# Decoder layer, last batch of the first stage: step sizes and sums in another order, part of the work in the next stage

## The reference

```
x = x + attention(layernorm(x))            # 16 heads of 32, 2 key/value heads, causal softmax
x = x + mamba(context, layernorm(x))       # selective scan over the context, gated by silu of the normed x
x = x + experts(layernorm(x))              # 16 experts, two chosen per token, and a shared one
```

```
c  = silu(conv4(in_proj(context)) + conv_b)         # 512 channels x 512 steps
dt_low, B, C = split(x_proj(c))                     # 16 rows each
dt = softplus(dt_proj(dt_low) + dt_b)               # 512 x 512
q, k, v = projections of layernorm(x)
state = state * exp(dt * A) + (dt * c) * B          # A = -exp(a_log), 16 states per channel; y = sum(state * C) + D * c
```

## Time and profile before

| | us |
|---|---|
| median of three runs | 1198.75 |
| profiled execution | 1197.57 |
| its span in the profile | 1195.8 |
| first stage, to the start of the second | 171.07 |
| second stage, to its last attention tile at 679.7 | 508.6 |
| the rest | 516.1 |

### The profile page before, as it was taken

The page is one execution under the profiler, slowest core; times in us unless marked ns, Lnnn a source line. Parts: engine busy times, 40 slices in busy tenths (PEclk is TensorE's granted clock), DMA queues, the critical chain, the costliest instruction groups (busy, mean ns, idle before and its releaser), DMA issues. The chain is left out here.

```text
span 1195.8 us, 18629 instructions
## 1 busy us (share of the span) xinstructions
PE 1072.8 (90%) x6368; PEld 641.9 (54%) x6368; DVE 808.5 (68%) x1199; ACT 666.1 (56%) x1438; POOL 672.2 (56%) x587
## 2 busy tenths in 40 slices
PE   7999928888888888888888899999999989999993
PEld 3444415655656665656656544544444456666651
DVE  5478769999999999999999567740680133323327
ACT  3566669999999999999999424202011022222210
POOL 1033269999999999999999640202043034444420
PEclk9999959999999999999999999999999999999997
DMA  6210001101111111112232123112225423333229
GB/s 211 90 37 19 13 15 36 37 32 32 36 36 37 37 32 32 37 36 72 80 100 70 58 85 106 68 38 70 71 72 205 162 88 125 125 130 127 69 73 367
DMA packets 51932, 94.74 MB, mean 79 GB/s; under 512 B 9918, under 2 KB 18110, under 8 KB 51840
## 3 DMA queue, kind: packets, MB, share of 16 engines
q1 hardware_dynamic: 44320, 72.82, 18.4%
q0 software_dynamic: 7520, 20.72, 5.3%
HBM read 74.51 MB, written 20.84 MB: 80 GB/s over the span
## 5 line engine op out<-in xcount | busy, mean ns | idle before, releaser
L604 POOL TENSOR_TENSOR w_all<-w_all 128x512 f32<-128x512 f32 x256 | 320.3, 1274 | 0.6 <-POOLq L96 0.3
L782 DVE TENSOR_TENSOR_SCAN w_all<-da,w_all 128x512 f32<-128x512 f32 x256 | 297.8, 1205 | 0.0
L716 ACT ACTIVATE da<-w_all,a_flat 128x512 f32<-128x512 f32 x256 | 180.2, 704 | 9.0 <-PEq L96 7.7
L683 PE MATMUL yb<-ident,w_all 128*128 128x128 f32 x1024 | 159.8, 279 | 21.0 <-DVE acc L790 21.0
L633 PE MATMUL sc<-w_all,attn 32*128 32x384 f32 (+3 forms) x512 | 105.0, 486 | 45.5 <-ACT w_all L724 22.8
L724 ACT ACTIVATE w_all<-sc,neg_max 128x128 f32<-128x128 f32 (+3 forms) x256 | 134.2, 540 | 15.0 <-DVE neg_max L774 13.9
L683 PEld LDWEIGHTS yb<-ident,w_all 128*128 128x128 f32 x1024 | 115.0, 141 | 45.4 <-issue 24.3
L1199 POOL TENSOR_TENSOR w_all<-w_all 128x512 f32<-128x512 f32 x24 | 29.4, 1226 | 165.0 <-ACT w_all L1396 165.0
L774 DVE TENSOR_REDUCE neg_max<-sc 128x2 f32<-128x256 f32 (+3 forms) x128 | 104.1, 813 | 24.1 <-PE sc L636 20.1
L733 ACT ACTIVATE w_all<-tb 128x256 f32<-128x256 f32 (+2 forms) x192 | 102.9, 536 | 22.6 <-PE tb L648 22.6
L1261 PE MATMUL pc<-w_all 128*128 128x512 f32 x256 | 112.1, 593 | 0.0
(11 more groups left out here) (198 smaller groups left out, 1679.1 us busy)
## 6 DMA issues: line engine op xcount, KB each, us to landing
w_all<-b_scratch SPq DMA_DIRECT2D x64, 256.0 KB, 3.3
w_all<-in_w_up SPq DMA_DIRECT2D x16, 512.0 KB, 5.4
w_all<-in_w_down SPq DMA_DIRECT2D x16, 512.0 KB, 6.6
w_all<-sorted_y SPq DMA_DIRECT2D x16, 512.0 KB, 10.9
attn<-in_x SPq DMA_DIRECT2D x4, 1024.0 KB, 7.4
w_all<-in_x SPq DMA_DIRECT2D x16, 256.0 KB, 4.0
norms<-attn SPq DMA_DIRECT2D x4, 1024.0 KB, 4.3
out_dram<-acc SPq DMA_DIRECT2D x16, 256.0 KB, 8.9
```

Of the source, the lines that this page charges most:

```text
L604: pool.tensor_tensor(dbu[:, k, :], keep["du"][i // N][:, k * T:(k + 1) * T], b_all[i % 2][:, :], ALU.mult).then_inc(pool_dbu.sem, pool_dbu ...
L683: last = pe.transpose(yb[which][:, k * P:(k + 1) * P], state[i % 2][:, k, t * P:(t + 1) * P], ident[:, :])
L716: act.activation(da[unit % 2][:, :], keep["dt"][i // N][:, k * T:(k + 1) * T], ACT.Exp, scale=keep["a_flat"][:, unit % (N * KD):unit % (N ...
L782: dve.tensor_tensor_scan(state[i % 2][:, k, :], da[unit % 2][:, :], dbu[:, k, :], 0.0, ALU.mult, ALU.add).then_inc(dve_scan.sem, dve_scan. ...
```

## The change

For the last batch (LAST = 3) of the first stage only, unless said otherwise:

- TensorE: after three of four query tiles the step rows, then at once the step sizes, then keys and values (into bank 0), the fourth query tile, the skip transposes (banks 1, 2, 5, 6), C, V. V's and C's transposes and the skip's are functions of their own, called for the other batches in the old order.
- The normalized x goes to `w_in` and `ctx_t` instead of `acc`, and the skip term to `xp` instead of `dt`'s tile, so that their new neighbours can write those.
- The step rows are copied by VectorE and not ScalarE.
- Abs reads the step sizes from PSUM with the bias in the instruction; the biased value for the sum is computed on VectorE after it.
- The sums, in all batches, are max(z, 0) - lost, ahead of the logarithm, and + ln behind it; 1 + e and lost alternate.
- exp(a_log) and a_flat are computed in the loop's second iteration.
- The fourth query tile's scaling, the skip copies and the C and V copies are at the end of ScalarE's stream.
- SyncE stores the B rows ahead of the keys' spreading.
- GpSimd's four products dt * c move into the second stage, one each in its steps 0 to 3.

```diff
+        def skipped(b, j):
+            return xc(b, j) if b < LAST else xp[:, j, TAPS - 1:]
+        def skip_bank(b, l):
+            return bank[l] if b < LAST else bank[(1, 2, 5, 6)[l]]
@@ sync: the last batch's rows before its keys @@
+                if b < B - 1:
+                    spread_keys(b)
...
                 sp.dma_start(d["b_rows"][b, :, :], rows[R:R + N, :]).then_inc(s_b.sem, s_b.tick(b))
+                if b == B - 1:
+                    spread_keys(b)
@@ gpsimd @@
-            weigh(B - 1)
@@ tensor @@
+                for m in range(3 if b == B - 1 else 4):
+                    query(b, m)
+                if b < B - 1:
+                    key_value(b)
+                step_rows(b)
+            steps(LAST)
+            key_value(LAST)
+            query(LAST, 3)
+            turn_skip(LAST)
+            turn_c(LAST)
+            turn_v(LAST)
-            tail(B - 1)
+            def steps(b):
...
+                else:
+                    pe.wait_ge(act_xt.sem, act_xt.upto(4 * b + 3))
+                    pe.wait_ge(dve_rows.sem, dve_rows.upto(0))
                 for j in four:
                     pe.matmul(bank[4 + j][:, :], w_dt4[j * DH:j * DH + R, j * P:(j + 1) * P], rows[j * DH:j * DH + R, :],
@@ scalar @@
             def exponent(b):
...
+                    else:
+                        act.wait_ge(pe_dt.sem, pe_dt.upto(4 * b + j))
+                        act.activation(ex[:, j, :], bank[4 + j][:, :], ACT.Abs, bias=dt_b[:, j:j + 1]).then_inc(act_abs.sem, act_abs.tick(4 * b + j))
...
+                if b == 0:
+                    act.wait_ge(s_rest.sem, s_rest.upto(6))
+                    act.activation(a_log[:, :, :], a_log[:, :, :], ACT.Exp).then_inc(act_alog.sem, act_alog.tick(0))
...
-            skip(B - 1)
-            exponent(B - 1)
-            logarithm(B - 1)
+            exponent(LAST)
+            logarithm(LAST)
+            scale_q(LAST, 3)
+            skip(LAST)
+            act.wait_ge(pe_v.sem, pe_v.upto(LAST))
+            copy_c(LAST)
+            act.activation(heads(LAST), bank[7][:, 0:NT * KVD].rearrange("p (t g c) -> p t g c", t=NT, g=KV), ACT.Copy)
@@ vector @@
             def time_bias(b):
                 for j in four:
                     dve.wait_ge(pe_dt.sem, pe_dt.upto(4 * b + j))
+                    if b == LAST:
+                        dve.wait_ge(act_abs.sem, act_abs.upto(4 * b + j))
+            def last_rows():
+                dve.wait_ge(pe_rows.sem, pe_rows.upto(LAST))
+                dve.wait_ge(s_b.sem, s_b.upto(LAST - 1))
+                dve.wait_ge(pe_dt.sem, pe_dt.upto(4 * LAST - 1))
+                dve.tensor_copy(rows[:, :], bank[5][:, :]).then_inc(dve_rows.sem, dve_rows.tick(0))
             def softplus_in(b):
+                plus_one(b, 0)
+                plus_one(b, 1)
+                lost(b, 0)
+                plus_one(b, 2)
+                lost(b, 1)
+                plus_one(b, 3)
+                lost(b, 2)
+                lost(b, 3)
+            def softplus_mid(b):
...
+                    dve.scalar_tensor_tensor(dt, dt, 0.0, ex[:, j, :], ALU.max, ALU.subtract).then_inc(dve_sum.sem, dve_sum.tick(4 * b + j))
             def softplus_out(b):
...
+                    dve.tensor_tensor(dt, dt, ln[:, j, :], ALU.add).then_inc(dve_dt.sem, dve_dt.tick(4 * b + j))
...
                 if b + 1 < B:
                     normalize(b + 1)
+                if b > 0:
+                    softplus_mid(b - 1)
+                if b == LAST:
+                    last_rows()
                 if b > 0:
                     softplus_out(b - 1)
-            heads_in(B - 1)
-            time_bias(B - 1)
-            softplus_in(B - 1)
-            softplus_out(B - 1)
+            time_bias(LAST)
+            keys(LAST)
+            softplus_in(LAST)
+            softplus_mid(LAST)
+            softplus_out(LAST)
@@ second stage, gpsimd @@
+            def last_batch(j):
+                dt, du = [keep[n][B - 1][:, j * T:(j + 1) * T] for n in ("dt", "du")]
+                pool.tensor_tensor(du, dt, du, ALU.mult).then_inc(pool_du.sem, pool_du.tick(j))
...
                 if g + 1 < UNITS:
                     weigh(2 * g + 3)
+                if g < KD:
+                    last_batch(g)
```

More of the change, by code:

```diff
@@ L179, in load_ctx, with spread_keys @@
                 sp.dma_start(ctx_t[:, :, :], d["ctx_t"][b, :, :].rearrange("(k p) t -> p k t", p=P)).then_inc(s_c.sem, s_c.tick(b))
+            def spread_keys(b):
+                sp.wait_ge(dve_kv.sem, dve_kv.upto(b))
+                for g in range(KV):
+                    for r in four:
+                        sp.dma_start(k_4[r * DH:(r + 1) * DH, b, g, :], kv_stage[g * DH:(g + 1) * DH, :]).then_inc(s_k.sem, s_k.tick((b * KV + g) * 4 + r))
             def column(name):
@@ L207, in _ @@
                     load_x(b + 2)
[L208 to L212, removed]
+                if b < B - 1:
+                    spread_keys(b)
+                if b < LAST:
+                    sp.wait_ge(act_rows.sem, act_rows.upto(b))
+                else:
+                    sp.wait_ge(dve_rows.sem, dve_rows.upto(0))
                 sp.dma_start(d["b_rows"][b, :, :], rows[R:R + N, :]).then_inc(s_b.sem, s_b.tick(b))
+                if b == B - 1:
+                    spread_keys(b)
                 if b == 0:
@@ L296, in tail, with query, key_value, step_rows @@
                                          start=True, stop=True).then_inc(pe_dt.sem, pe_dt.tick(4 * b + j))
+            def query(b, m):
+                if b > 0:
+                    pe.wait_ge(act_du.sem, act_du.upto(4 * (b - 1) + m))
+                else:
+                    pe.wait_ge(act_xp.sem, act_xp.upto(m))
+                group(bank[m][:, :], [(wq[:, k, m * P:(m + 1) * P], x_n_t(b, k)) for k in four]).then_inc(pe_q.sem, pe_q.tick(4 * b + m))
+            def key_value(b):
+                pe.wait_ge(s_kvw.sem, s_kvw.upto(3))
+                if b == LAST:
+                    pe.wait_ge(act_q.sem, act_q.upto(4 * b))
+                group(kv_bank(b)[:, :], [(w_kv[:, k, :], x_n_t(b, k)) for k in four]).then_inc(pe_kv.sem, pe_kv.tick(b))
+            def step_rows(b):
+                pe.wait_ge(pool_wx.sem, pool_wx.upto(3))
+                for k in four:
+                    pe.wait_ge(act_silu.sem, act_silu.upto(4 * b + k))
+                    last = pe.matmul(bank[5][:, :], w_x4[:, k, :], u(b, k), start=(k == 0), stop=(k == 3))
+                last.then_inc(pe_rows.sem, pe_rows.tick(b))
             pe.wait_ge(s_const.sem, s_const.upto(6))
@@ L306, in _ @@
                 if b > 0:
-                    tail(b - 1)
+                    turn_v(b - 1)
+                    turn_c(b - 1)
+                    turn_skip(b - 1)
+                    steps(b - 1)
                 for k in four:
@@ L433, in heads_in, with keys @@
                 dve.tensor_copy(
-                    keep["v"][:, :, :].rearrange("p (b g) (t c) -> p b t g c", g=KV, t=NT)[:, b, :, :, :],
+                    heads(b),
                     bank[7][:, 0:NT * KVD].rearrange("p (t g c) -> p t g c", t=NT, g=KV)).then_inc(dve_v.sem, dve_v.tick(b))
+            def keys(b):
+                dve.wait_ge(pe_kv.sem, pe_kv.upto(b))
+                if b > 0:
+                    dve.wait_ge(pe_v.sem, pe_v.upto(b - 1))
+                    dve.wait_ge(s_k.sem, s_k.upto(4 * KV * b - 1))
+                dve.tensor_scalar(kv_stage[:, :], kv_bank(b)[:, :], b_kv[:, 0:1], None, ALU.add).then_inc(dve_kv.sem, dve_kv.tick(b))
             def time_bias(b):
@@ L488, in _ @@
                     softplus_in(b - 1)
-                dve.wait_ge(pe_kv.sem, pe_kv.upto(b))
-                if b >= 1:
-                    dve.wait_ge(pe_v.sem, pe_v.upto(b - 1))
-                if b > 0:
-                    dve.wait_ge(s_k.sem, s_k.upto(4 * KV * b - 1))
-                dve.tensor_scalar(kv_stage[:, :], bank[4][:, :], b_kv[:, 0:1], None, ALU.add).then_inc(dve_kv.sem, dve_kv.tick(b))
+                if b == 1:
+                    dve.wait_ge(act_alog.sem, act_alog.upto(0))
+                    dve.tensor_scalar(keep["a_flat"][:, :].rearrange("p (n k) -> p k n", k=KD), a_log[:, :, :], -1.0, None, ALU.mult)
+                if b < B - 1:
+                    keys(b)
                 if b + 1 < B:
```

113 lines of the change are left out of this document (62 added, 51 removed).

## The result

The changed kernel takes 1188.99 us (median of four, 1187.5 to 1190.77) against 1198.44 before (median of four, 1197.11 to 1200.22): ratio 0.9918, 95% interval 0.9903 to 0.9933, 9.5 us faster. A second group of runs gave 1187.59 against 1199.26, ratio 0.9911, 0.9897 to 0.9925. The forecast was 1186.3 in a range of 1183.5 to 1190.5, a gain of 12.4 on the 1198.75 known then. By the two ratios the gain is 9.8 and 10.7 us, so 1.7 to 2.6 us of the forecast one are missing. The first profile is of the slowest execution of its four (1190.77), the second of the median one of its five (1187.59), so the second stands closer to the medians.

A forecast was written before the change was run, and what follows sets the result against it. Bound: a chain through several engines ending the first stage, before a barrier; the second stage is near full on VectorE and GpSimd. 14.0 saved less 1.6 charged gives 12.4 us: 1197.57 to 1185.2, plus 1.2 for the median, 1186.3; range 1183.5 to 1190.5.

The forecast's parts named there:

- The chain: First stage's end: step rows through VectorE's last sums end at 156.8; second stage starts 14.0 us sooner.
- I add 0.2: Softplus sums at the first stage's end: GpSimd's batch 2 products, running beside them, cost VectorE 0.2 us.
- my ends: VectorE's end in the first stage: 156.2 with no contention, 158.1 if each meeting costs a full GpSimd product.
- My low end, 156.2: VectorE's end in the first stage if GpSimd's products cause no contention at the sums.
- Table load: Second stage's start: Exp table load ahead of the first decay holds the first scan until about +2.0 us.
- The opening: Second stage's first units: GpSimd's four products cost a 1.6 us stall, with the table load's 0.95 inside it.
- TensorE's clock: Second stage's opening: at full clock VectorE comes 1 to 2 us sooner but waits for GpSimd; nothing taken.
- one or two such waits: Sign: VectorE's scan stalls once or twice on GpSimd near +20 to +30 us, adding to 1 to 2 us.
- the +12: Sign of being wrong: half clock lasts past +12 us in the second stage.
- The count of GpSimd: Second stage's opening: unit 11 becomes GpSimd's 18th operation, done at +22.2 us, where VectorE took it at +20.6.
- rival C: Second stage: TensorE's clock stays at half, each us losing 0.43; 45 us more gives 1205.6, slower; chance 0.03.
- a_log and a_flat, batches 0 to 2: Rest of the first stage: moved exp(a_log) and a_flat, and re-ordered sums, cost nothing; 1.3 us at most without cover.

The follow-up runs named there:

- f3: f2 (spaced products, Exp table loaded ahead of the barrier) plus added matmuls to hold TensorE's clock full: 1183.90 us, ratio 0.9870.
- f4: f1 (spaced products) plus added matmuls, seven ending the first stage and 3, 2, 1 in the second's first steps: 1184.22 us, ratio 0.9875.
- e4: Changed kernel with GpSimd's four batch 2 products moved into second-stage steps 16, 24, 32 and 40: 1184.90 us, ratio 0.9880.
- f1: Changed kernel with GpSimd's products of batches 2 and 3 both in the second stage, one every eighth step from 8 to 64: 1185.94 us, ratio 0.9888.
- f2: f1 plus a one-column Exp ending ScalarE's first-stage stream, so the table loads ahead of the barrier: 1186.09 us, ratio 0.9891.
- e5: e3 plus 3, 2 and 1 matmuls behind the scores of second-stage steps 0, 1 and 2, for full clock: 1186.98 us, ratio 0.9906.
- e6: e5 with GpSimd's four last-batch products left out (computes something else, for time only): 1184.41 us, ratio 0.9882.
- e2: Changed kernel with GpSimd's four last-batch products left out (computes something else, for time only): 1188.26 us, ratio 0.9908.
- e3: Changed kernel with seven matmuls added behind TensorE's last first-stage transposes, to keep it busy to the barrier: 1187.87 us, ratio 0.9909.
- e8: Kernel before with only GpSimd's four last-batch products moved to second-stage steps 0 to 3: 1195.23 us, ratio 0.9972.
- e1: Changed kernel with GpSimd's four last-batch products put back at the end of the first stage: 1192.65 us, ratio 0.9947.

## Why the prediction was right, and where it was off

The time lies in the range, 2.7 us above the forecast in the first group and 1.3 in the second. The first stage came by the mechanism forecast, with one term too small. What the second stage charges came by another mechanism than the one I had, and that the number is near in the second profile (2.1 us for my 1.6) is luck.

- *The chain* was right link by link: rows 14.0 us behind the first query group (forecast 13.8), Abs 16.5 (16.6), keys copied 20.8 (20.9), first sum 20.9 (21.0), VectorE last, ScalarE 1.2 us ahead of it (1.0).
- *The term that was mis-sized* is the contention at the softplus sums, "I add 0.2": it cost 2.9 us. VectorE ended 32.6 us behind the first query group, where my ends were 29.9 and 31.8; without contention it was 29.7 (f3, f4). My low end, 156.2, doesn't follow from my own sum, which without the 0.2 gives 156.6, or 30.3. I had let the products begin at 142.3 with the sums they wait for. But GpSimd was still at its skip products until 145.1, in 9.5 us instead of 4.8, beside a VectorE that now works on where it had paused for 5 us; so the products fell on the sums. That they cost it is shown by e4, f3 and f4; why the skip products took twice their time is read from the rows alone.
- *Table load*: the first scan +2.26 us instead of +1.50, forecast +2.0; taking it away gives 0.3 us of the opening at full clock (f4 to f3) and 1.0 at half (f1 to f2). The Trainium skill (ScalarE: Activation LUTs, What ACT_TABLE_LOAD costs) would have put 1.38 us of drain on top; the first decay starts 1.29 us after its load, at 160.15, so the measurement decides for the row.
- *The opening* was forecast 1.6 us longer and was 2.1 and 4.2 longer, for another reason: TensorE's clock, for which I took nothing. This is the step that failed. I argued that a wait for GpSimd would hold VectorE all the same, and expected one or two such waits; there was none, and half clock lasted to +22.5 and +16.4 us, past the +12 that I had named as a sign of being wrong. The count of GpSimd was exact (22.2 us, seen in e5, whose opening of 25.2 us at full clock is nearly the 23.45 + 1.6 that I had forecast), but at half clock TensorE is later still. This was rival C's mechanism in a small form: half clock lasted 12.5 us longer than before in the first profile and 6.4 in the second. At rival C's rate of 0.43 us for each that would be 5.4 and 2.8 us; e5 and e6 put a price on it.
- *After the opening* I had taken nothing, and the second profile bears it out (485.2 us in both kernels from unit 12 on). The first profile's 1.1 us more go with the stretch at half clock at 662 us; e2, e3, e4, e8, f2 and f3 have such a stretch as well, and no run tells what brings it.
- *a_log and a_flat, batches 0 to 2* cost nothing: the first query group of batch 3 starts at 125.7 to 126.8 in all kernels, 126.32 before.
- *Share of the parts*: of 11.9 us in the stage, 4.8 are GpSimd's products (e1), the other 7.1 the order of TensorE and VectorE, ScalarE's part and a_log together, which no run here takes apart.

## What to carry to other kernels

When work moves off the end of a stage, look at what the engine that gave it up did before: its earlier, unmoved work now lies beside the new critical sums, and what the two cost each other is to be measured before it is called small: here 2.9 us for the 0.2 on paper. Count a queue in operations to the point of need, but take the later of that count and of every other engine's at its real clock: two delays of like size hide each other, and removing either one alone shows next to nothing.

## What the runs showed of the hardware

- TensorE's clock fell and rose at times that didn't follow the stages: half from 153.7 to 181.05 before, 153.8 to 181.1 after, 155.2 to 175.65 in the second profile, with the restart at 171.1, 158.6 and 159.3. In 158.6 to 180 it was at half with TensorE busy 16.9 of 21.4 us; in e5, with seven matmuls ahead of the barrier and six in the pauses of the first three steps, it was at full throughout 150 to 180.
- Seven of the fourteen profiles have one more short stretch at half clock near 660 us, amid steady work of TensorE (662.4 to 665.8 in the first one after); their second stages took 0.7 to 1.1 us more behind the opening than the others'.
- What VectorE lost beside GpSimd's products depended on the operation. Four TENSOR_SCALAR of 128x512 between SBUF tiles took 1.42 us, and two took 2.73 beside the products; one of 128x64 took 0.22 alone (e8) and 1.32 beside them. Four SCALAR_TENSOR_TENSOR took 2.49 us beside them, the same as without them (f3), and it was GpSimd that was slower there (1.64 a product). In the changed kernel, though, the first SCALAR_TENSOR_TENSOR behind the two TENSOR_SCALAR took 1.76 (L542). VectorE's scans and GpSimd's products (1.23 each) didn't slow each other.
- From the last engine's end to TensorE's first matmul of the next stage the barrier took 0.3 us (158.29 to 158.61 after, 158.24 to 158.53 in f3).
